# Self-attention with one pool of seven PSUM banks, a new order of the unit and a shorter lead

## The reference

```python
q = qkv[:, :, 0].transpose(0, 2, 1, 3)
k = qkv[:, :, 1].transpose(0, 2, 1, 3)
v = qkv[:, :, 2].transpose(0, 2, 1, 3)
attn = jnp.einsum('bhnd,bhsd->bhns', q, k) * SCALE
attn = jax.nn.softmax(attn, axis=-1)
o = jnp.einsum('bhns,bhsd->bhnd', attn, v)
x = x + g_sa * (o.transpose(0, 2, 1, 3).reshape(B, N, D) @ sa_proj_w + sa_proj_b)
```

## Time and profile before

| what | us |
|---|---|
| median of 3 runs | 4469.03 (4458.99 to 4475.24) |
| the profiled execution, its own time | 4450.84 |
| its span, first to last instruction | 4449.0 |
| PE / DVE / ACT / POOL busy | 3853.9 / 2132.4 / 1968.4 / 560.0 |
| first to last exponential of the first self-attention | 842.57 to 1037.15 |

### The profile page before, as it was taken

How to read it: one execution, slowest core, us unless ns; L and a number is a source line. 1 busy time by engine, 2 the same in 40 slices (tenths; PEclk the granted TensorE clock), 3 DMA queues, 4 the chain that set the end, 5 groups by cost and what they waited for, 6 DMA issues and landing times.

```text
span 4449.0 us, 65095 instructions
## 1 busy us (share of the span) xinstructions
PE 3853.9 (87%) x19345; PEld 2093.7 (47%) x19345; DVE 2132.4 (48%) x3376; ACT 1968.4 (44%) x3402; POOL 560.0 (13%) x312
## 2 busy tenths in 40 slices
PE   7999996888888896889888878888889788888888
PEld 4555554334633563346334733355346333463355
DVE  1112121673286445742673437535754376437544
ACT  2122121475357332754474326642754247436642
POOL 1000000001400320013002300031023000130040
PEclk9999998897889777997897879978988689789977
DMA  3000002202310225011401240024011320140022
GB/s 102 25 10 19 10 29 82 59 2 56 77 38 2 61 51 114 2 47 39 86 2 42 69 110 6 18 58 95 2 33 46 91 58 16 42 111 4 4 58 60
DMA packets 119992, 204.30 MB, mean 46 GB/s; under 512 B 21014, under 2 KB 75740, under 8 KB 119676
## 3 DMA queue, kind: packets, MB, share of 16 engines
q1 hardware_dynamic: 90868, 175.04, 16.6%
q10 hardware_dynamic: 28808, 25.17, 1.8%
HBM read 76.82 MB, written 9.44 MB: 19 GB/s over the span
## 4 chain that ended last, share of the span: by engine, by line
issue 63%; PE 25%; POOL 6%; DMA 2%; SPq 1%; DVE 1%; ACT 1%; ACTq 0%; POOLq 0%; DVEq 0%
PE ps L643 23%; POOL hidl L1653 2%; SPq L564 1%; DMA out<-x 1%; POOL x L1644 1%; POOL small L1592 1%; PE ps L1058 1%; POOL W1h L1662 1%; POOL W2h L1662 1%; DMA x_after_block<-x 0%; DVE mx L1550 0%; POOL W1l L1664 0%; POOL W2l L1664 0%; POOL hTl L1599 0%; DMA gw<-in_L_gate_w 0%
## 5 line engine op out<-in xcount | busy, mean ns | idle before, releaser
L1315 ACT ACTIVATE probs<-ps 128x512 f32<-128x512 f32 (+1 forms) x2176 | 1190.2, 631 | 501.8 <-PE ps L643 497.3
L1554 DVE TENSOR_REDUCE mxh<-ps 128x2 f32<-128x1024 f32 x1024 | 1201.0, 1219 | 316.6 <-PE ps L643 306.9
L643 PE MATMUL ps<-qk 63*128 63x512 f32 (+1 forms) x4096 | 942.3, 472 | 232.1 <-DVE mxh L1554 129.7
L643 PEld LDWEIGHTS ps<-qk 63*128 63x128 f32 (+1 forms) x4096 | 461.3, 194 | 945.2 <-DVE mxh L1554 366.5
L643 PE MATMUL ps<-probs,v 128*32 128x512 f32 (+1 forms) x4864 | 716.6, 664 | 3.8 <-ACT probs L1315 3.8
L1592 POOL TENSOR_TENSOR small<-small 128x4 f32<-128x4 f32 x64 | 67.0, 1047 | 3506.5 <-DVE small L1360 3506.5
L643 PE MATMUL ps<-hT,slot 128*128 128x512 f32 x448 | 257.9, 727 | 79.2 <-ACT hT L1128 72.4
L1541 DVE SCALAR_TENSOR_TENSOR split<-ps,cols,split 128x512 fp32r<-128x512 f32 x112 | 84.1, 751 | 326.0 <-ACT split L1281 326.0
L643 PE MATMUL ps<-kc,qk 63*128 63x78 f32 x1536 | 193.1, 387 | 48.2 <-DVE mx L1550 20.8
L643 PE MATMUL ps<-slot,hT 128*128 128x256 f32 x896 | 218.1, 390 | 9.3 <-ACT hT L1326 9.3
L1550 DVE TENSOR_REDUCE mx<-ps 128x4 f32<-128x312 f32 x384 | 175.3, 482 | 88.2 <-PE ps L643 85.1
(11 more groups left out here) (191 smaller groups left out, 4882.1 us busy)
## 6 DMA issues: line engine op xcount, KB each, us to landing
qk<-split SPq DMA_DIRECT2D x192, 256.0 KB, 5.3
qk<-split SPq DMA_DIRECT2D x288, 128.0 KB, 2.6
qk<-fixed SPq DMA_DIRECT2D x20, 1024.0 KB
slot<-in_L_w SPq DMA_DIRECT2D x8, 1024.0 KB, 7.6
slot<-in_L_fc_w SPq DMA_DIRECT2D x8, 1024.0 KB, 13.3
adw<-in_L_adaln_w SPq DMA_DIRECT2D x4, 1536.0 KB, 6.6
xin<-in_x ACTq DMA_DIRECT2D x5, 1024.0 KB, 5.4
x_after_block<-x ACTq DMA_DIRECT2D x20, 256.0 KB, 2.2
```

The lines of the kernel that those rows point to most:

```text
L643: return pe.matmul(out, lhsT, rhs, start=start, stop=stop)
L1315: ins = act.activation(dst, src, ACT.Exp, scale=SCALE)
L1554: dve.tensor_reduce(mxh[:, z, t, j // 2, j % 2, :], ps[:, a:a + 2, :], AX.X, ALU.max, negate=True).then_inc(dve_done, M.add(dve_done, name))
```

## The change

Six things change.

1. In self-attention every step that needs a bank (A, S, P, V, T, R, M, OT, aT, o) takes it from one pool of banks 0 to 6: the bank, or for A the pair of neighbours, that was given out longest ago, where a pair counts as given out somewhat later (`shared`). PV keeps bank 7.
2. A unit is now S0, S1, OT if due, PV, S2, S3, and then two A steps side by side. A maxima entry that is no A (both, M) follows at once where the list has it. `lead` is 20 A steps ahead of the first unit (23 before, with two more entries), and unit `u` brings the count to `20 + 2u + 2`. For the second `(g, n)` both and M come one A earlier.
3. Ahead of the units: in self-attention R goes from the head of the module to behind the tenth A, and the first A stands between the projections of the second half. The 24 stacking transfers go out in the order (g0, n0), (g1, n0), then after the second half's projections the other 18. `aT` and `o` in the tail come one unit later.
4. SP no longer sets the constant rows of side 0 for L1sa in every block; L3ca's own setting of that side is left in place, and one transfer ahead of the loop serves the first block. In L2sa the load of W2 (1 MB) goes behind the 24 stacking transfers.
5. In cross-attention the maxima of a half are sent by two transfers of eight rows instead of eight transfers of two rows.
6. In cross-attention three A steps stand between the projections of the second half, the first M follows A step 17 instead of 16, and eleven A steps instead of six lie among the units.

```diff
         for g in range(GROUPS):
             for n in range(NH):
                 scores = [("A", g, n, t, 2 * c + i) for i in range(NH) for t in range(TPH) for c in range(2)]
+                ahead = 1 if (g, n) == (0, 1) else 2
                 both, turned = turn[:1], turn[1:]
-                maxima += scores[:2] + both + scores[2:4] + turned + scores[4:]
+                if ahead == 1:
+                    maxima += both + scores[:1] + turned + scores[1:]
+                else:
+                    maxima += scores[:2] + both + scores[2:4] + turned + scores[4:]
                 turn = [("both", g, n), ("M", g, n)]
...
         def more(upto):
+
             nonlocal taken
-            upto = min(int(upto), len(maxima))
-            put(tag, *maxima[taken:upto])
-            taken = max(taken, upto)
+            while taken < len(maxima) and (maxima[taken][0] != "A" or sum(m[0] == "A" for m in maxima[:taken]) < upto):
+                put(tag, maxima[taken])
+                taken += 1
...
-        more(GH * TPH + 6 + 3)
-        ahead, rate, lag = taken, (GH * TPH + 2) / NT, 2
+        more(10)
+        put(tag, ("R",), ("add",))
+        lead, lag = GH * TPH + 4, 2
+        more(lead)
...
             if u < end:
-                more(ahead + rate * (u + 0.5))
                 put(tag, *[("S",) + units[u] + (j,) for j in range(2)])
...
             if u < end:
-                more(ahead + rate * (u + 1))
                 put(tag, *[("S",) + units[u] + (j,) for j in range(2, GH)])
+                more(lead + 2 * u + 2)
...
     def cross_attention(tag, follow):
-        put(tag, *queries(1), ("add",))
-        maxima = [("A", i // TPH, n, i % TPH, 0) for n in range(NH) for i in range(GROUPS * TPH)]
-        put(tag, *maxima[:GROUPS * TPH], ("M", 0, 0), *maxima[GROUPS * TPH:-6])
-        last = maxima[-6:] + [("M", 0, 1)]
+        first = [("A", i // TPH, 0, i % TPH, 0) for i in range(GROUPS * TPH)]
+        last = [("A", i // TPH, 1, i % TPH, 0) for i in range(GROUPS * TPH)]
+        put(tag, ("P", "q", 0, 1), *first[:3], ("P", "q", 1, 1), ("add",), *first[3:], *last[:1], ("M", 0, 0), *last[1:5])
+        last = last[5:] + [("M", 0, 1)]
...
+                    def shared(count):
+
+                        b = min(range(8 - count), key=lambda i: max(used[i:i + count]))
+                        used[b:b + count] = [max(used) + (1 if count == 1 else 3)] * count
+                        return tuple(range(b, b + count))
+
                     def small():
+                        if not alone:
+                            banks = shared(2 if kind == "A" else 1)
+                            return banks[0], banks
                         rings["small"] += 1
-                        if not alone and kind not in ("T", "R", "mod"):
-                            b = 2 * (rings["small"] % 2)
-                            return b, (b, b + 1) if kind == "A" else (b,)
...
                     def single():
+                        if not alone:
+                            return shared(1)
                         rings["single"] += 1
-                        if alone:
-                            return (2 + rings["single"] % 4,)
-                        maxima_done = kind == "S" and PASS.index((tag, "M", GROUPS - 1, NH - 1)) < PASS.index(name)
-                        return ((4, 5, 6, 1, 3)[rings["single"] % 5] if maxima_done else 4 + rings["single"] % 3,)
+                        return (2 + rings["single"] % 4,)
...
+                def stack_all_maxima(tag, n):
+
+                    sp.wait_ge(act_done, upto(act_done, (tag, "M", 0, n)))
+                    for e in range(2):
+                        sp.dma_start(qk[STACK * e + MAXROW:STACK * e + MAXROW + 1, 0, n].bitcast(F32).rearrange("r g c k -> r (g c) k"),
+                                     mrow[e:HEADS:2, n * HALF:(n + 1) * HALF]
+                                     ).then_inc(maxima_stacked[0][n], M.add(maxima_stacked[0][n], (tag, e), LOADED))
...
                 sp.wait_ge(mm_done, upto(mm_done))
-                for side in range(2):
-                    set_rows("L1sa", side)
+                set_rows("L1sa", 1)
```

More of the change, by code:

```diff
@@ L598, in _ @@
                 stack_self("L1sa")
+                for g, n in BLOCK_ORDER:
+                    stack_maxima("L1sa", g, n)
                 sp.wait_ge(pool_done, upto(pool_done, ("row", "L1sa")))
@@ L616, in _ @@
                     set_rows("L2sa", side)
+                stack_self("L2sa")
                 sp.dma_start(W2, wide(T["L2_fc2_w"])).then_inc(slot_loaded[3], M.add(slot_loaded[3], "L2mlp", LOADED))
-                stack_self("L2sa")
+                for g, n in BLOCK_ORDER:
+                    stack_maxima("L2sa", g, n)
                 set_key_rows("L2ca", "L2sa")
@@ L1015, in _ @@
                         if (kt, j) == (0, 0):
[L1016 removed]
+                            of = 0 if cross else g
+                            pe.wait_ge(maxima_stacked[of][n], upto(maxima_stacked[of][n], (tag, 1)))
                         if cross:
@@ L1061, in _ @@
                         n, c = step[1:]
-                        if alone:
-                            a, banks = small()
-                            _, act_was, dve_was = take(name, act=name, banks=banks)
-                        else:
-                            a, act_was, dve_was = take(name, act=name, banks=single())
+                        a, banks = small()
+                        _, act_was, dve_was = take(name, act=name, banks=banks)
                         pe.wait_ge(act_done, upto(act_done, *act_was))
```

90 lines of the change are left out of this document (49 added, 41 removed).

## The result

The changed kernel takes 4713.94 us (4693.89 to 4727.57, 4 runs) against 4465.5 (4458.99 to 4475.24, 4 runs) of before: a ratio of 1.0551, interval 1.0502 to 1.06. It is slower, by 248 us, where the prediction had slower by 115 and a range that ended at 4680. Of these, 25 us lie in L0, ahead of the first self-attention; behind L0 the two traces differ by 248 us.

The account below looks back on a forecast made before the run. No engine is full: waits for banks and PE's in-order steps set the unit. -74 + 146 + 86 - 12 + 12 - 18 - 8 = +132 on the profiled 4450.84 gives 4583, forecast as 4580; range 4470 to 4680.

Parts of the forecast that it names:

- The new unit: Self-attention units with A steps: from 3.16 to 2.96 us each, -74 us over eight modules.
- The reading of the banks: In 54 of 54 units the first A needs the pair that the second A of the unit before had.
- The wait at the turn: Self-attention, six of eight turns a module: PE waits for the maxima directly behind M, +3.0 us each, +146 for 48.
- The clock at the turn: PE's idle gap at each of 48 turns drops the clock to 0.50: 1.8 us a turn, +86.
- the other short gaps' stretches: Half-clock stretches behind PE's other short idle gaps before the change: said to last the same 3.4 and 6.8 us.
- The rival by that section's rule of thumb: Gaps as short as the turns' don't lower the clock, or it returns in time: without the 86, 4497; chance 0.18.
- Cross-attention: Twelve cross-attention modules: fewer SP issues and moved A steps give -0.7 us each, -8 in all.
- three A fill DVE's idle time: Cross-attention: a gain from three A steps, within the -0.7 us a module.
- Five A move among units that PE bounds, which takes back most: Cross-attention: five moved A steps take back most of the gain, leaving -0.7 us a module.
- The heads: Heads of the self-attentions: L1sa -3 us each, -12 for four; L2sa +3 each, +12 for four.
- The heads of blocks: Start of blocks two to four: 1 MB less on SP frees ACT's small loads, -6 us each, -18.
- one rival's value: Rival that the clock stays low longer, 3.4 us a turn: 77 more, 4660; chance 0.08.

Follow-up runs that it names:

- the busy kernel: The changed kernel with PE computing 12 throwaway matmuls while it waits for the maxima at six turns of a self-attention; 4598.82 us, ratio 1.0314 to before.

## Why the prediction was right in kind and wrong in size

- **The new unit: right.** 2.96 us forecast, 2.95 to 2.96 measured in nearly every unit without a turn, and the lead of 24, which takes the turns away, made it a gain. The reading of the banks was a little too strong: followed through `shared`, the first A has just the pair of the second A before it in 36 of 53 units of L1sa, and in the other 17 one bank of it. Either holds it until that A is reduced, so the loop is the same.
- **The wait at the turn: right.** Six a module, +3.0 forecast, 3.05 measured with the clock held up; 48 of them are 146.
- **The clock at the turn: right in kind, a little too small.** 1.8 forecast, 2.1 measured: 101 instead of 86. All 48 turns paid. One or two of the units behind a turn are still longer at times (3.0 to 3.7 us). The reading that the other short gaps' stretches last "the same" as 3.4 and 6.8 us doesn't hold for all: behind some of them the trace of before has 24 to 48 us at 0.50. Nor does every short gap bring the clock down: in the changed kernel three of 20 gaps of 1.8 to 2.5 us had none of this behind them. For the turns the trace bears out the mechanism that the Trainium skill describes under "HAM oscillation — how this bites in real kernels" (page "TensorE: Matmul & The Clock Gate"), and the busy kernel shows its price. The rival by that section's rule of thumb, 4497, falls.
- **The first two units of a module: missing, +17.** The sum had 2.96 us for each; they take 4.3 to 4.8 and 3.0 to 3.9, at half clock, 2.1 more in each of eight modules. The first S now waits as well, 4.8 to 10.6 us:

```profile
863.90 1.75 PE L675 MATMUL ps<-qk 64*128 64x512 f32 x6 [5.31 <-DMA qk<-mrow]
```

That wait explains only a part. Before, the first S didn't wait, and yet the clock was at 0.50 when every module's exponentials began, and the first two units took 3.8 and 3.0 to 4.2; with lead 24, where the first S of an L1sa waits 0.6 us at most, they take 3.3 and 3.7 to 3.9. How much the wait adds beyond this was not tried.
- **Cross-attention: wrong, the largest miss.** Forecast -8, measured about +32 (36 in the exponentials, -3 ahead of them). The step that failed is "three A fill DVE's idle time": it was put down as a gain without a cost, but the three A stand ahead of the second half's last projection of queries, and in L2ca and L3ca M came 2.4 and 5.0 us later. "Five A move among units that PE bounds, which takes back most" was right as far as it went: they take back 2.9 of the 3.0 that L1ca gains ahead. In L2ca and L3ca nothing was gained ahead that they could take back. By module the loss is none in L1ca, some 3 us in L2ca and some 5 in L3ca.
- **The heads: wrong in the reason.** Forecast 0 in sum, measured +12 (L1sa -9 against -12, L2sa +21 against +12). I priced W2 at 5 us of data ahead of the maxima; W2 is 1.6 of the loss. The 18 transfers of L2sa were priced from 1220, which is 25 us behind its first projection, on the step that the second half would be ready some 3 us sooner. It was not: the seventh transfer left 29 to 30 us behind the first projection, after some 8 us in which SP stood idle, and the order of the stacking cost 7.6 us.
- **The heads of blocks: wrong.** Forecast -18. One megabyte less in SP's queue took 0.6 us off the gap of 14.50, and two megabytes more a further 3.0. ACT's ctxT does not leave sooner in any of them. I had taken a queue that was busy at the time for the cause of the wait.
- **L0: not forecast.** 25 us lie ahead of L1sa's first projection, and they aren't the change's doing as far as its instructions go: up to SP's loads of L1sa's weights, which go out at 769.42 instead of 744.74, no instruction differs. The last section tells what they are. The other executions of the changed kernel weren't traced, so how much of this is in the median isn't known.

In sum +132 forecast and +273 in the profiled execution: -74 and +146 as said, clock at the turns +101 instead of +86, first units +17, cross +32 instead of -8, heads +12 instead of 0, blocks' heads -2 instead of -18, L0 +25, and 16 of small stretches. By medians it is 248 against 115. The last turn's wait, which the lead of 24 left standing, is in no term either. The forecast of 4580 also left out what its own text names: +132 on the median of before, 18 us above the trace, is 4601. The range failed because it ended at one rival's value: the upper bounds of the terms, which the text gave, add up to well above 4680. L0 alone doesn't save it; without those 25 us the median is still above 4680.

## What to carry to other kernels

A chain of 3.4 us through three engines and a transfer must be issued ahead of its user by more than its length; the engine in order that meets the wait directly behind the chain's first step pays it all, with everything queued behind, and then pays again in clock. Before a number like a lead is cut, count the steps between producer and waiting consumer in the emitted order, for every iteration. The same holds at the end of the list: the last turn has no later work to hide behind unless some is kept for it. And steps moved along an engine that is full cost the same in their new place; what can change is what they covered in the old one, and what now waits behind them in the new one.

## What the runs showed of the hardware

The same instructions of L0 took different times in executions of different kernels, and the granted clock tells them apart. Where its first block ends and its second begins, before and after both fall to half clock. Of the changed kernel the first row, of before the second, each from where the clock falls:

```profile
208.60:229.00 20.40, 17.16 (x56) 12.72 (x55) 9.17 (x32) 4.75 (x7) 2.72 (x3) 0.50 0.24 77
```

```profile
213.20:233.60 20.40, 15.87 (x77) 10.97 (x77) 7.75 (x29) 10.26 (x27) 7.28 (x6) 0.83 0.17 53
```

In the changed kernel the clock stays at 0.50 for the whole 20.4 us; before, it is back after 6.8, a mean of 0.83. The same four matmuls, the last of the first block's output, take 2.08 us in the one and 1.13 in the other:

```profile
214.61 2.08 PE L675 MATMUL ps<-outw,rT 128*128 128x256 f32 x4
```

```profile
208.80 1.13 PE L643 MATMUL ps<-outw,rT 128*128 128x256 f32 x4
```

It comes back at the start of the two later blocks of the changed kernel (392.90 to 413.40 and 577.20 to 597.70, at 0.50 too) and costs 3 to 4 us each time; the rest of the 25 us gathers in steps of 1 to 4 us elsewhere in L0. Over the 14 traces the first projection of L1sa starts at 785.5 to 792.4 us in six and at 804.9 to 821.2 in eight. The kernel before and the two built on it are all in the first group, but so are three of those built on the changed kernel, so the program doesn't decide it alone; with one trace of each, whether it has a part isn't known. Parts of a few tens of us in a sum over one profiled execution can be of this kind.

I had also not expected that throwaway matmuls pay: 12 of them in each of 48 waits made the whole kernel some 2% faster (3805.5 against 3911.1 us behind L0).
